# Attention with heads of 32: row sums of the probabilities taken once per unit, division on the chip; and more places for side work in the causal attention

## The reference

```python
xn, yn = _ln(x, lnx_g, lnx_b), _ln(y, lny_g, lny_b)
q = jnp.einsum('bsc,hcd->bhsd', xn, wq)
k = jnp.einsum('btc,hcd->bhtd', yn, wk)
v = jnp.einsum('btc,hcd->bhtd', yn, wv)
a = jax.nn.softmax(jnp.einsum('bhsd,bhtd->bhst', q, k) * D ** (-0.5), axis=-1)
if causal:
    a = a * mask            # after the softmax: the row sums run over all keys
o = jnp.einsum('bhst,bhtd->bhsd', a, v)
x_out = x + o @ li1_w + li1_b
```

## Time and profile before

| stretch, us from the span's start | PE busy | granted PE clock |
|---|---|---|
| L0 attention, 130 to 700 | 490.53 | 0.80 |
| L2 a1 ticks, 1457 to 1852 | 379.62 | 0.99 |
| behind a1, 1852 to 1873 | 0.23 | 0.57 |
| L2 a2 ticks, 2151 to 2526 | 360.41 | 0.98 |
| behind a2, 2526 to 2546 | 0.31 | 0.61 |
| whole span, 3992.9 | 2947.2 | 0.825 |

### The profile page before, as it was taken

The page is one execution under the profiler, slowest core; times in us unless marked ns, Lnnn a source line. Parts: engine busy times, 40 slices in busy tenths (PEclk is TensorE's granted clock), DMA queues, the critical chain, the costliest instruction groups (busy, mean ns, idle before and its releaser), DMA issues. The chain is left out here.

```text
span 3992.9 us, 44779 instructions
## 1 busy us (share of the span) xinstructions
PE 2947.2 (74%) x17140; PEld 1646.0 (41%) x17140; DVE 1897.7 (48%) x3008; ACT 1480.7 (37%) x1967; POOL 962.5 (24%) x1021
## 2 busy tenths in 40 slices
PE   4998995648859379996738999497989976870233
PEld 2333332623326234443633444285877862320121
DVE  3534542646724534441663444254234225644798
ACT  1444444416632135442413555243324323660111
POOL 2122322022222125555121333400000010222233
PEclk7767987768969789998866999798999986995555
DMA  5344552044510001111010111101101115531000
GB/s 124 81 93 103 110 111 63 1 81 96 111 51 0 25 6 44 44 45 61 1 31 6 50 44 47 53 1 48 43 30 51 47 45 90 118 78 40 2 10 11
DMA packets 133043, 209.43 MB, mean 52 GB/s; under 512 B 41696, under 2 KB 66272, under 8 KB 132704
## 3 DMA queue, kind: packets, MB, share of 16 engines
q1 hardware_dynamic: 87776, 136.94, 15.2%
q0 software_dynamic: 45056, 69.64, 6.1%
HBM read 134.53 MB, written 71.83 MB: 52 GB/s over the span
## 5 line engine op out<-in xcount | busy, mean ns | idle before, releaser
L1590 DVE TENSOR_REDUCE L_mx<-bank_t 128x2 f32<-128x1024 f32 (+3 forms) x512 | 564.6, 1122 | 501.4 <-PE bank_t L1414 278.3
L1791 ACT ACTIVATE L_P<-bank_t 128x1024 f32<-128x1024 f32 (+2 forms) x512 | 478.4, 949 | 461.2 <-PE bank_t L1428 292.5
L1590 DVE TENSOR_REDUCE L2a_mx<-bank_t 128x2 f32<-128x1024 f32 x256 | 312.9, 1224 | 471.9 <-PE bank_t L1391 470.7
L1791 ACT ACTIVATE L2a_P<-bank_t 128x1024 f32<-128x1024 f32 x256 | 262.2, 1024 | 258.8 <-PE bank_t L1403 258.8
L1414 PE MATMUL bank_t<-L_KS,L_QS 48*128 48x512 f32 (+2 forms) x1024 | 268.2, 527 | 107.1 <-DMA L_QS<-L_spill_q_halves 85.9
L1428 PE MATMUL bank_t<-L_QS,L_KS 50*128 50x512 f32 (+2 forms) x1024 | 242.8, 477 | 74.4 <-DVE L_mx L1590 55.6
L1459 PE MATMUL bank_o<-L_P,L_V 128*32 128x512 f32 (+3 forms) x2048 | 289.4, 641 | 4.9 <-ACT xn L1795 3.3
L1414 PEld LDWEIGHTS bank_t<-L_KS,L_QS 48*128 48x128 f32 x1024 | 109.5, 212 | 408.2 <-issue 277.3
L1463 PE MATMUL bank_o<-L2a_P,ones 128*32 128x512 f32 x1024 | 271.4, 607 | 0.0
L1364 PE MATMUL bank_t<-ident,xn 128*128 128x128 f32 x224 | 50.0, 395 | 217.7 <-DVE xn L1548 204.6
L1679 DVE TENSOR_TENSOR L2g_act_low<-ctxT,L2g_act_high 128x512 fp32r<-128x512 f32 x96 | 66.5, 693 | 293.4 <-ACT L2g_act_high L1829 293.4
(11 more groups left out here) (438 smaller groups left out, 6700.5 us busy)
## 6 DMA issues: line engine op xcount, KB each, us to landing
L_KS<-L_spill_k_halves SPq DMA_DIRECT2D x192, 128.0 KB, 4.2
L_QS<-L_spill_q_halves SPq DMA_DIRECT2D x192, 128.0 KB, 4.8
L_spill_raw<-xn POOLq DMA_DIRECT2D x64, 256.0 KB, 2.4
L2a_spill_raw<-xn POOLq DMA_DIRECT2D x64, 256.0 KB, 2.4
L2g_raw<-in_L_ffn_h_blocks SPq DMA_DIRECT2D x32, 512.0 KB, 3.5
L_spill_k_halves<-L_hi SPq DMA_DIRECT2D x32, 256.0 KB, 2.0
L_spill_k_halves<-L_lo SPq DMA_DIRECT2D x32, 256.0 KB, 2.3
L_spill_q_halves<-L_hi SPq DMA_DIRECT2D x32, 256.0 KB, 4.8
```

Of the source, the lines that this page charges most:

```text
L1590: e.tensor_reduce(neg, s.tile[:, :, 0:n_keys], AX.X, ALU.max, negate=True).then_inc(sem(s.done), 1)
L1791: e.activation(s.at.Pr[s.pb][:, :, q0:S], s.tile[:, :, q0:S], ACT.Exp, scale=s.at.scale).then_inc(sem(s.exp), 1)
```

## The change

With heads of 32 (a1 and a2):

- A Values block serves both pairs: its four groups are the V products of four heads, with no ones. There is one block per two ticks, 4 per unit instead of 8, and `lag` goes from 2 to 1.
- `SumTiles` adds the probability tiles (128x1024, float32) of a pair over the four key tiles, three adds per pair, six per unit. In a2 four of the six are on POOL and two on DVE; in a1 two are on POOL and four on DVE.
- `SumKeys`, one block of four matmuls with ones per unit, sums over the 128 rows that are left. It goes to `bank_m` and stands at the head of `chores`. `SumsOut` (ACT) copies it to SBUF, four `InvertPart` (DVE, 128x128) take reciprocals, and `Scale` (POOL, 128x512) multiplies. `CopyGroup` stays, once per unit. All the DMAs of the division are gone.
- Buffers: `NP_` 7 instead of 6 probability tiles in a2, 6 diagonal tiles instead of 4, first pass 5 ticks more than a unit ahead instead of 4; the first passes alternate between the two pairs.

In L0, whose jobs begin with a causal one, a chore may now run at either tick of a block (`any_tick`). L1 and L3 keep their order.

```diff
-            at.GP = 2 if D == 16 else 1
+            at.GP = 2
...
-            lead = unit_ticks + (6 if D == 16 else 4)
-            lag, gap, after_mm, after_dma = (1, 2, 1, 2) if D == 16 else (2, 1, 0, 1)
+            lead = unit_ticks + (6 if D == 16 else 5)
+            lag, gap, after_mm, after_dma = (1, 2, 1, 2) if D == 16 else (1, 1, 0, 1)
...
+            any_tick = D == 32 or jobs[0]["mode"] == "causal"
...
+            def add_up(un, s, place, part):
...
+                i, e, first = summed[un.n, s]
+                engine = "gpsimd" if place == 1 + s or (place == 3 and not upper) else "vector"
+                done = due("summed_" + engine)
+                other = at.Pr[first[0]] if place == 1 else sums[i]
+                add(SumTiles(engine, sums[i], other, at.Pr[part[0]],
+                             [part[1], first[1], sums_free[i]] if place == 1 else [part[1], e], done))
...
+                if place == TB - 1 and s == n_pairs - 1:
+                    chores.insert(0, lambda: sum_keys(un))
+
+            def sum_keys(un):
...
+                add(SumKeys([sums[m[0]] for m in mine], bank, [misc.free[i_bank], *[m[1] for m in mine]], mm))
...
+                out = SumsOut(inv[i][:, :], bank, [mm, inv_free[i]], copied)
+                later(1, lambda: add(out))
+                misc.free[i_bank] = copied
+                for k in range(TB):
+                    later(2 + k, lambda k=k: invert_part(un, i, k, copied))
+
+            def invert_part(un, i, k, e):
+                done = due("sums_inverted")
+                add(InvertPart(inv[i][:, k * P:(k + 1) * P], [e], done))
+                if k == TB - 1:
+                    later(1, lambda: scale(un, i, done))
...
             def copy_group(un, g, e_o):
...
+                if D == 32:
+                    add(CopyGroup(at, un, g, raw[r], [e_o, raw_free[r]], done, None, None, None, None))
+                    o_free[0], un.i_raw, un.raw, un.raw_done = done, r, raw[r], done
+                    return
...
+                            if D == 32:
+                                later(2, lambda un=un, p=p, place=place, part=parts[-1]: add_up(un, p, place, part))
...
-                            run_due(chore=p == at.GP - 1)
+                            run_due(chore=any_tick or p == at.GP - 1)
...
-                            if st.D == 32 and i == 0:
-                                mm = e.matmul(bank_o[row + 32:row + 64, :], ones[:, 0:32], s.at.Pr[pb][:, c, :],
-                                              start=s.first, stop=s.last, tile_position=(0, row + 32))
...
+                elif kind is SumKeys:
+                    pe.wait_ge(*s.after)
+                    for p in range(2):
+                        for c in range(2):
+                            row = 32 * (2 * p + c)
+                            mm = e.matmul(s.bank[row:row + 32, :], ones[:, 0:32], s.sums[p][:, c, :], start=True, stop=True,
+                                          tile_position=(0, row))
```

More of the change, by code:

```diff
@@ L97 @@
 SumsIn = namedtuple("SumsIn", "at un rec den_dram after landing")
+SumTiles = namedtuple("SumTiles", "engine dst a b after done")
+SumKeys = namedtuple("SumKeys", "sums bank after mm")
+SumsOut = namedtuple("SumsOut", "dst bank after done")
+InvertPart = namedtuple("InvertPart", "part after done")
+Scale = namedtuple("Scale", "ot raw inverse after done")
 Inverse = namedtuple("Inverse", "at un rec after done rec_dram out_after landing")
@@ L346, in attention @@
             raw = [xn[:, 1, 2 * i:2 * i + 2, :].rearrange("p t c -> p (t c)") for i in range(2)]
[L347 to L350 removed]
+            n_back = 2
+            if D == 16:
+                back = [sb(scope, f"{tag}_back{i}", [P, 2, S]) for i in range(n_back)]
+                rec = [sb(scope, f"{tag}_rec{i}", [P, H * S // P]) for i in range(2)]
+            else:
+                sums = [sb(scope, f"{tag}_sums{i}", [P, 2, S]) for i in range(4)]
+                inv = [sb(scope, f"{tag}_inv{i}", [P, S]) for i in range(2)]
+            at.diag = [sb(scope, f"{tag}_diag{i}", [P, 2, P]) for i in range(6)] if upper else None
             at.mx = [sb(scope, f"{tag}_mx{i}", [P, TB, st.q_of, st.slots]) for i in range(2)]
@@ L545, in probabilities, with scale @@
                 return pb, e_p, i_d, e_m
+            def add_up(un, s, place, part):
+                if place == 0:
+                    i = n_sums[0] % 4
+                    n_sums[0] += 1
+                    summed[un.n, s] = [i, None, part]
+                    return
[5 more added lines that the diff above has]
+                             [part[1], first[1], sums_free[i]] if place == 1 else [part[1], e], done))
+                summed[un.n, s][1] = done
+                for pb in (part[0], first[0])[:2 if place == 1 else 1]:
+                    P_free[pb] = P_free[pb] + [done]
+                if place == TB - 1 and s == n_pairs - 1:
+                    chores.insert(0, lambda: sum_keys(un))
+            def sum_keys(un):
+                i_bank, bank = misc.take()
+                mm, copied = due("keys_summed"), due("sums_out")
+                i = un.n % 2
+                mine = [summed.pop((un.n, s)) for s in range(n_pairs)]
+                add(SumKeys([sums[m[0]] for m in mine], bank, [misc.free[i_bank], *[m[1] for m in mine]], mm))
+                for m in mine:
+                    sums_free[m[0]] = mm
+                out = SumsOut(inv[i][:, :], bank, [mm, inv_free[i]], copied)
[8 more added lines that the diff above has]
+                    later(1, lambda: scale(un, i, done))
+            def scale(un, i, e):
+                done = due("divided")
+                add(Scale(OT[:, un.u, :], un.raw, inv[i][:, :], [e, un.raw_done, OT_free[0]], done))
+                raw_free[un.i_raw] = inv_free[i] = OT_ready[un.u] = done
+                last_unit(un)
             def values(un, g, kt, place, parts):
@@ L601, in divide @@
                     later(2, lambda: chores.extend(steps))
-            flat = [(un, s, qt) for un in units for s in range(n_pairs) for qt in range(TB)]
+            if D == 16:
+                flat = [(un, s, qt) for un in units for s in range(n_pairs) for qt in range(TB)]
+            else:
+                flat = [(un, s, qt) for un in units for qt in range(TB) for s in range(n_pairs)]
             n_max = [0]
@@ L1602, in vector_program @@
                     e.tensor_tensor(low, mx, high.bitcast(F32), ALU.subtract).then_inc(sem(s.done), 1)
+                elif kind is SumTiles and s.engine == "vector":
+                    dve.wait_ge(*s.after)
+                    e.tensor_tensor(s.dst[:, :, :], s.a[:, :, :], s.b[:, :, :], ALU.add).then_inc(sem(s.done), 1)
+                elif kind is InvertPart:
+                    dve.wait_ge(*s.after)
+                    e.reciprocal(s.part, s.part).then_inc(sem(s.done), 1)
                 elif kind is Inverse:
@@ L1792, in scalar_program @@
                                  scale=s.at.scale).then_inc(sem(s.exp), 1)
+                elif kind is SumsOut:
+                    act.wait_ge(*s.after)
+                    e.activation(s.dst, s.bank, ACT.Copy).then_inc(sem(s.done), 1)
                 elif kind is CopyGroup:
@@ L1908, in gpsimd_program @@
                     pool.latest = s.lo
-                elif kind is CopyGroup:
+                elif kind is SumTiles and s.engine == "gpsimd":
+                    pool.wait_ge(pool.latest, *s.after)
+                    e.tensor_tensor(s.dst[:, :, :], s.a[:, :, :], s.b[:, :, :], ALU.add).then_inc(sem(s.done), 1)
+                    pool.latest = s.done
+                elif kind is Scale:
+                    pool.wait_ge(pool.latest, *s.after)
+                    e.tensor_tensor(s.ot, s.raw, s.inverse, ALU.mult).then_inc(sem(s.done), 1)
+                    pool.latest = s.done
+                elif kind is CopyGroup and s.landing is not None:
                     D = s.at.D
```

31 lines of the change are left out of this document (17 added, 14 removed).

## The result

The changed kernel took 4200.42 us in the middle of four runs (4198.72 to 4216.92), the kernel before 3994.18 on the same chip. The ratio is 1.0533, with a 95% interval of 1.0485 to 1.0582. The change makes the kernel 5.3% slower, some 213 us. The forecast was 4195, and 4200 is inside the range and on the side that was forecast. The profiled execution of the changed kernel has a span of 4215.1 us; its clock over the whole span is 0.806, against 0.825.

The account below looks back on a forecast made before the run. L2's plain tick was taken as bound by a loop from PE to DVE and ACT, not PE's work. The profiled 3995 plus 112 for stalls, tails and L0, plus 94 for clock, gave 4201, 4195 by the median; range 4055 to 4320.

Parts of the forecast that it names:

- What bounds the kernel: L2 plain ticks: a loop from PE to DVE and ACT sets 2.37 us; without the block PE's idle grows to 1.2.
- The wait in a2: In a2 PE stands 4.1 us at SumKeys for POOL's add; +7.0 per unit, +84 over 12 units.
- The wait in a1: In a1 PE stands 2.4 us at SumKeys for DVE's add; +5.3 per unit, +52 after the side work's -12.
- a rule beside its sum: DVE and POOL lock each other out: +0.6 at a1's add before SumKeys, 12 units; sum about 4205 to 4220.
- -12 for each stage: In a1 and a2, about 12 V and output projections per stage lose the Values block beside them, saving at most 1.06 each.
- Tails: Behind the last Values block the chain of six DMAs goes; 8.5 us left in a1, about 10.5 in a2, -22 together.
- L0: Moved chores in L0: first-pass waits for DVE +17, shorter stack waits -7; +10 in all, bounds -50 and +50.
- L0 gains: Rival: L0's five stack waits shrink, some 120 us run at full clock, -40 to -60, L2's clock stays; about 4045, 6%.
- The clock in L2: Half clock behind 12 SumKeys waits each in a2 (4.3 us) and a1 (3.5); +94, bounds 0 and some +300.
- Faster: Rival: in L2 SumKeys finds its sums ready, so no stall; 3944 by the median, 6%.
- full clock kept: Rival: SumKeys stalls in a1 and a2 as forecast, but the clock stays and the 94 go; 4101, 18%.
- about the same: Rival: all cancels, full clock, stalls half as long, L0 at its lower bound; within 40 us of 3989, 4%.

Follow-up runs that it names:

- e5: Changed kernel without its adds, SumKeys summing only the last key tile's probabilities, so divisors differ from the reference's; 3936.29 us, ratio 0.989 to the kernel before.
- e1: Kernel before with only the L0 edit, a chore may run at either tick of a block; 3940.53 us against 3971.94, ratio 0.992.
- e3: Changed kernel with two (a1) or three (a2) blocks of useless matmuls ahead of SumKeys' wait; 4130.81 us, ratio 1.0402 to the kernel before.
- e8: Kernel before with four blocks of useless matmuls ahead of each of four PE stack waits in L0; 3951.71 us, ratio 0.9954.
- e9: Changed kernel with SumKeys two ticks later, reciprocals spread over ticks, all six adds of a unit on DVE; 3941.09 us, ratio 0.9933 to the kernel before.
- e6: Changed kernel with SumKeys two ticks later and a unit's four reciprocals in ticks of their own; 3963.44 us, ratio 0.9978 to the kernel before.

## Why the prediction was right, and where it was not

**What bounds the kernel.** Right. The plain tick kept its 2.37 us, and PE's idle time in it grew from 0.18 to 1.16 us, as forecast (1.2). e5 shows it from the other side.

**The wait in a2.** Right: 4.21 for 4.1, and 3.9 to 4.2 in all twelve units. The Q projection behind it waited 1.22 for the copy of the sums, for the forecast 1.4. A plain unit, from one Q projection to the next (2303.43 is one's start; the two behind 2334.51 start at 2368.25 and 2402.18), takes 33.8 us against 21.8: +12.0, where the forecast has 7.0 and 4.3. That the sum fits so well is in part luck, since the half clock stands elsewhere in the unit. The forecast put most of its 4.3 on the Q projection (+3), which ran at full clock in all twelve units. In its place it was the K projection. The two ticks with reduction, reciprocal and add took 1.9 us more for the forecast 2.1, but PE then waits 2.4 us for DVE's last reduction, in 8 of the 12 units, and behind that wait the clock falls:

```profile
2347.26 1.72 DVE L1681 TENSOR_TENSOR L2a_sums<-L2a_sums,L2a_P 128x1024 f32<-128x1024 f32 x1
2348.90 1.21 DVE L1666 TENSOR_REDUCE L2a_mx<-bank_t 128x2 f32<-128x1024 f32 x1
2350.21 0.79 PE L1462 MATMUL bank_t<-L2a_K_high,L2a_Q_high 32*128 32x512 f32 x2 [2.38 <-issue]
2354.09 2.08 PE L1424 MATMUL bank_m<-L2a_KT,L2a_wk 128*128 128x512 f32 x2
```

The profile names no releaser here ("issue"), but the reduction ends at 2350.11, 0.10 us ahead of PE's start. The tick with the K projection takes 5.88 us in these units, and 3.18 in the other four and in the kernel before: +2.7, a second fall of the clock in each of these units, which the forecast does not have.

**The wait in a1.** Mechanism right, 0.5 us short: 2.87 for 2.4. The forecast took the undisturbed add of 1.23; the add ahead of this `SumKeys` takes 1.78, because POOL's `K_low` runs to 1584.40:

```profile
1583.14 1.26 POOL L1991 TENSOR_TENSOR L2a_K_low<-xn,L2a_K_high 128x512 fp32r<-128x512 f32 x1 [2.77 <-ACT L2a_K_high L1860]
```

```profile
1583.70 1.78 DVE L1681 TENSOR_TENSOR L2a_sums<-L2a_sums,L2a_P 128x1024 f32<-128x1024 f32 x1
```

The Trainium skill ("SBUF — State Buffer", "Who interferes with whom") says that a DVE instruction with two SBUF inputs contends with a GpSimd instruction that reads SBUF, and that this is an exclusive lock. The trace agrees: 0.70 us of wait and the 1.16 of an undisturbed add are 1.86, and the add took 1.78. The prediction had this as a rule beside its sum, with +0.6 at this place, and should have put it into the sum instead of its typical row, which was of operations that seldom met.

**Side work in ticks without a block, "-12 for each stage".** This step failed. The V projections did save: in a1 their four ticks took 4.05 us each before and take 4.06, 3.05, 3.84 and 3.05 now, -2.2 in each of three units. But the tick with a batch's second output projection grew from 6.64 to 10.21 us, +3.6 in each of two units. The forecast looked only at PE. The second output projection needs the bank that DVE empties with `XT`, and this instruction now stands behind a reciprocal and an add:

```profile
1608.35 5.41 PE L1424 MATMUL bank_m<-L2a_li,ctxT 128*128 128x256 f32 x16 [3.67 <-DVE XT L1690]
```

```profile
1605.64 0.94 DVE L1684 RECIPROCAL L2a_inv<-L2a_inv 128x128 f32<-128x128 f32 x1
1606.50 1.20 DVE L1681 TENSOR_TENSOR L2a_sums<-L2a_P 128x1024 f32<-128x1024 f32 x1
1607.62 0.68 DVE L1690 TENSOR_TENSOR XT<-L_Y,bank_m 128x512 f32<-128x512 f32 x1
```

Before, the same wait was 0.78 us. The two effects cancel, so the term was about 0 in a1, not -12. In a2, where the V ticks saved only some 0.5 us per unit and the second output projection went from 6.64 to 10.15, it was a loss.

**Tails.** They gave -16 instead of -22: there are 11.7 and 13.2 us from the last Values block to the output projection (1962.73 and 2764.07), where 8.5 and 10.5 were forecast; `SumKeys` and what is behind it run at half clock there too.

**L0.** The sum had the wrong sign: +10, against -32 us timed (e1). The waits that it is made of were partly right. Waits of the first pass for `L_mx` went from 18.3 to 35.9 us, +17.6 for the forecast +17; the stack waits only fell from 11.1 to 8.8, -2.3 for the forecast -7, and the longest of them even grew:

```profile
242.61 0.47 PE L1485 MATMUL bank_t<-L_KS,L_QS 48*128 48x128 f32 x2 [4.05 <-DMA L_QS<-L_spill_q_halves]
```

The clock, which the text named as a mere bound, decided it: 110 to 640 us ran at 0.89 instead of 0.80. The low clock between 228 and 288 us was on record, and its price was not put into the sum. The rival "L0 gains" was nearest, with -40 to -60. Its reason, stack waits that shrink below 2.2 us, held for all but this one, and behind this one the clock was back within 6 us.

**The clock in L2.** The mechanism is shown by e3: PE idle lowers the clock, and filling the idle time gives part of it back. The size can be estimated from the ticks, with e3's ticks at full clock as the measure. In a2 these are 6.45 us with `SumKeys`, 5.32 with the Q projection and 3.18 with the K projection, and the changed kernel's twelve units take 8, 17 and 22 us more, 47 together. In a1 (5.1 to 5.5, 5.21 and 3.63 us) they take 8, 29 and 21 us more, 58 together; there too the K ticks are long, 5.1 to 6.7 us, in 8 of 12 units, behind waits of 1.8 us and more. By this estimate the clock cost about 105 us where the forecast has 94, but spread otherwise: 43 of them at K projections, which the forecast does not have, and less than forecast behind `SumKeys`.

**Sum.** Up to the last Q projection a1 lost 113 us, for 106 by the forecast's 8.8 per unit, and a2 131 for 136 by its 11.3. The last four units, for which the forecast had nothing, added 20 and 14 us; their waits at `SumKeys` are up to 5.7 us. With the -12 that did not come, a1 was 39 short and a2 21. L0 hid this. "Faster", "full clock kept" and "about the same" did not happen. The lower end of the range, 4055, doesn't follow from the prediction's own words, which give 4101-35 = 4066; the measured time is far from either.

## What to carry to other kernels

An engine that is busy 96% of a stretch is not its bound if the next tick starts on another engine's word: ask how long a tick lasts with the work gone. Before an instruction with a wait goes on the engine that feeds all others, follow its producer's queue, and ask what stands ahead there; two ticks later the same block waited for nothing. And a change that makes the engine wait can pay twice, once for the wait and once for the half clock behind it; what comes right behind each new wait, and how long it would take at half clock, belongs in the sum.

## What the runs showed of the hardware

- Useless matmuls in an idle stretch of PE made the kernel faster twice: 64 of them in L0 by 0.46% (e8), and two or three blocks of four in each `SumKeys` wait by 1.3% of the kernel before (e3). Behind a wait of 0.75 us a block kept full speed (1.06 us), behind 2.87 us it mostly ran at half (1.94).
- How long the clock stays down varies. Behind a stack wait of 3.01 us it stood at 0.50 for some 60 us with PE busy all the time (before), behind 3.15 us (e1) and 4.05 us (the changed kernel) for less than 10. And it fell without a long wait, behind 0.81, 0.21 and 0.57 us (e9, 1517 us).
- A 128x1024 add on DVE with both inputs in SBUF takes 1.16 us alone and 1.72 us in the median beside such adds on POOL; POOL's 128x512 product took 2.13 instead of 1.29 behind a DVE add. Handing POOL's adds to the fuller engine made the kernel 0.45% faster (e6 to e9), all of it in a2.
